# A decoder layer with routed experts: opening order, store pieces, rounding order and the summing of group 7, changed together

## What is computed

```python
x = layernorm(x + linear_attention(x))           # rotary q and k, sums over 64 tokens, W_out, + x
x = layernorm(x + cross_attention(ctx, x))       # queries from x, keys and values from ctx and x, 16 heads of 64
logits = x @ Wg + bg                             # 8 experts, the best 2 of each token, softmax over them
y_e = gelu(x @ W1[e] + b1[e]) @ W2[e] + b2[e]    # D_FF = 512
out = layernorm(x + p_1 * y_1 + p_2 * y_2)       # p_1 + p_2 = 1
```

## Time and profile before

| | |
|---|---|
| median of 3 runs | 1443.15 us (1439.3 to 1445.73) |
| the profiled execution, its own time | 1446.45 us |
| its span, first to last instruction | 1444.3 us |
| PE busy | 1382.8 us (96%) |
| ACT, DVE, POOL busy | 1171.3, 1038.3, 1000.1 us |
| share of the chain of waits on PE, DVE, "another core or an unknown queue" | 75%, 9%, 5% |
| expert tiles, from the first `hidden` to the last | 1132.3 to 1411.2 us |

### The profile page before, as it was taken

How to read it: one execution, slowest core, us unless ns; L and a number is a source line. 1 busy time by engine, 2 the same in 40 slices (tenths; PEclk the granted TensorE clock), 3 DMA queues, 4 the chain that set the end, 5 groups by cost and what they waited for, 6 DMA issues and landing times.

```text
span 1444.3 us, 37673 instructions
## 1 busy us (share of the span) xinstructions
PE 1382.8 (96%) x10833; PEld 1302.3 (90%) x10833; DVE 1038.3 (72%) x3702; ACT 1171.3 (81%) x4154; POOL 1000.1 (69%) x1543
## 2 busy tenths in 40 slices
PE   5799999999999999999999999999999989999996
PEld 4699999999999999999999999999998879988993
DVE  4566888887888887888888888787766655445664
ACT  2579999989998989998888999988987666666765
POOL 4445777777777777777777777777755554456775
PEclk9999999999999999999999999999999989999998
DMA  3211111211111211111211111127101557777894
GB/s 97 56 39 38 46 46 49 63 46 48 46 46 51 61 46 48 46 47 48 59 49 46 48 46 48 52 58 130 37 9 63 162 168 224 221 233 235 292 292 150
DMA packets 130962, 129.65 MB, mean 90 GB/s; under 512 B 11810, under 2 KB 115112, under 8 KB 130760
## 3 DMA queue, kind: packets, MB, share of 16 engines
q1 hardware_dynamic: 114328, 106.84, 26.1%
q0 software_dynamic: 8832, 16.94, 3.5%
q10 hardware_dynamic: 7600, 3.48, 0.8%
HBM read 70.83 MB, written 57.30 MB: 89 GB/s over the span
## 4 chain that ended last, share of the span: by engine, by line
PE 75%; DVE 9%; another core or an unknown queue 5%; issue 4%; ACT 3%; POOL 2%; DMA 1%; DVEq 0%; SPq 0%; ACTq 0%; POOLq 0%
PE ps_s L1633 15%; PE ps_o L1649 14%; PE ps_pT L1659 7%; PE ps_u L1688 4%; PE ps_u L1689 4%; PE ps_u L1690 4%; PE ps_t L1673 4%; PE ps_t L1670 4%; PE ps_t L1671 4%; DVE score_lo L1156 2%; ACT probs L815 2%; PE ps_t L1891 1%; PE ps_o L1891 1%; DVE wqT L1489 1%
## 5 line engine op out<-in xcount | busy, mean ns | idle before, releaser
L815 ACT ACTIVATE probs<-ps_s,neg_max 128x128 f32<-128x128 f32 x1024 | 362.7, 366 | 114.4 <-DVE neg_max L1167 114.1
L550 POOL TENSOR_TENSOR probs_n<-probs,inv_sum 128x512 f32<-128x512 f32 x256 | 267.2, 1044 | 93.8 <-DVE inv_sum L1173 91.5
L1633 PE MATMUL ps_s<-kvT,u_sb 128*128 128x128 f32 x2048 | 275.7, 278 | 0.1
L1649 PE MATMUL ps_o<-value_w,tT 128*128 128x128 f32 x2048 | 260.0, 275 | 1.1 <-ACT tT L833 1.0
L1633 PEld LDWEIGHTS ps_s<-kvT,u_sb 128*128 128x128 f32 x2048 | 254.3, 192 | 6.8 <-ACT u_sb L807 0.4
L1649 PEld LDWEIGHTS ps_o<-value_w,tT 128*128 128x128 f32 x2048 | 244.0, 192 | 1.7 <-ACT tT L833 1.4
L1178 DVE TENSOR_TENSOR pT_lo<-ps_pT,pT_hi 128x512 fp32r<-128x512 f32 x256 | 175.0, 684 | 64.9 <-ACT pT_hi L824 64.0
L694 POOL DMA_INDIRECT y_rows<-wvT,f_x x142 | 142.9, 1007 | 106.1 <-DVE wvT L1496 76.3
L563 POOL DMA_INDIRECT x_rows<-routed,pos_i x128 | 139.2, 1087 | 101.1 <-issue 93.3
L815 ACT ACTIVATION_READ_ACCUMULATOR probs<-ps_s,neg_max 128x1 f32 x1024 | 207.8, 203 | 0.0
L1167 DVE TENSOR_REDUCE neg_max<-ps_s 128x4 f32<-128x512 f32 x256 | 177.0, 691 | 34.1 <-PE ps_s L1633 25.9
(11 more groups left out here) (290 smaller groups left out, 3623.5 us busy)
## 6 DMA issues: line engine op xcount, KB each, us to landing
u_sb<-in_expert_w SPq DMA_DIRECT2D x71, 578.0 KB
x_rows<-pad_row SPq DMA_DIRECT2D x66, 520.0 KB, 4.8
f_x<-x_rows SPq DMA_DIRECT2D x71, 130.0 KB
tT<-y_rows SPq DMA_DIRECT2D x16, 512.0 KB
x_raw<-in_x SPq DMA_DIRECT2D x64, 64.0 KB, 1.7
c_raw<-in_ctx_in SPq DMA_DIRECT2D x64, 64.0 KB, 2.0
out<-value_w ACTq DMA_DIRECT2D x12, 256.0 KB, 2.5
y_rows<-wvT,f_x POOLq DMA_INDIRECT x142
```

What stands on the lines that cost most here:

```text
L550: nc.gpsimd.tensor_tensor(probs_n[:, sl], probs[:, sl], inv_sum[:, sl, :].rearrange("p (u o) -> p u o", o=1).to_broadcast([P, UP, P]), ALU ...
L815: last = nc.scalar.activation(probs[:, sl, j], ps_s[sl][:, j * P:(j + 1) * P], ACT.Exp, bias=neg_max[:, sl, j:j + 1], accum_out=sums[:, sl ...
L1633: last = nc.tensor.matmul(ps_s[sl][:, j * P:(j + 1) * P], u_sb[:, c // 2, BT * p + b, h:h + 2].rearrange("p h s -> p (h s)"), kvT[:, c, 2 ...
L1649: last = nc.tensor.matmul(ps_o[:, 0:D], tT[:, (p + 1) % 2, h], value_w[:, h], start=(h == 0), stop=(h == H - 1))
```

## The change

1. **Opening.** Scores of units 0 and 1 of the first tile move from period 0 into the opening, between pieces of folded query rows, with their `row_max`, `exps`, `inverse_sum` and the first `scale`; the preparation of tile 4 (`stats`, `in_rstds`, `in_hats`, `x_low`) moves ahead, `project(4)` and `turn_queries(4)` move into period 0.
2. **Stores.** Result row numbers are permuted so that a partition holds four rows that follow each other in the output: a store writes 2 KB per partition in one piece instead of four of 512 B. Three small instructions make the numbers in the opening.
3. **Rounding order.** For expert tiles ACT rounds the weights before the rows; DVE's `result` is split in `biased` (line 1489's work) and the rest, and DVE's order becomes `rest_weights(i + 1)`, `biased(i - 1)`, `rest_rows(i + 1)`, `result(i - 1)`. PE's `hidden` takes the low weights before the low rows. The second table of tiles (`list_rows`, `tile_rows`, `tile_table`) is made two tiles later.
4. **Group 7.** `BESIDE` = 7 groups are summed by POOL beside the tiles; group 7 joins the groups that PE sums after the last tile.

```diff
+    BESIDE = HALF_GROUPS - 1
-    IN_AT = [HALF_TILES + X_SLOTS + 7 * g // 2 for g in range(HALF_GROUPS)]
+    IN_AT = [HALF_TILES + X_SLOTS + 7 * g // 2 for g in range(BESIDE)]
-    out_z = out.rearrange("(t b) s d -> t (b s) d", b=BT)
+    out_z = out.rearrange("(g b) s d -> g (b s) d", b=ZT * BT).rearrange("g (p c) d -> g p c d", c=ZT)
...
-                sp.dma_start(out_z[bass.ds(g * ZT, ZT), :, :].rearrange("t p d -> p t d"), e_out[:, q]).then_inc(s_out[q], 16)
+                sp.dma_start(out_z[g], e_out[:, q]).then_inc(s_out[q], 16)
...
-            for i in range(NF + 5):
-                if i < NF:
-                    result_out(i)
+            for i in range(NF):
+                result_out(i)
...
-            for g in range(HALF_GROUPS, NZ):
+            for g in range(BESIDE, NZ):
                 out_rstds(g)
...
                 if i + 1 < NF:
+                    upper_weights(i + 1)
                     upper_rows(i + 1)
-                    upper_weights(i + 1)
...
-            def result(i):
-                q = i % RING
+            def biased(i):
                 dve.wait_ge(f_y_ps, i + 1)
                 dve.wait_ge(f_y_done, count(TB * i - TB))
                 nc.vector.tensor_tensor(f_yb[:, i % 2], F_Y[i % 2].rearrange("p (b d) -> p b d", d=D),
...
+            def result(i):
+                q = i % RING
                 dve.wait_ge(y_routed[q], 16 * TB * (i // RING))
...
             def ffn(i):
                 if i + 1 < NF:
-                    rest_rows(i + 1)
                     rest_weights(i + 1)
                 if i:
+                    biased(i - 1)
+                if i + 1 < NF:
+                    rest_rows(i + 1)
+                if i:
                     result(i - 1)
...
             project(2)
             turn_queries(3)
             latents_part(4)
+            score(0, 0, 0)
+            turn_x(4)
             project(3)
-            turn_x(4)
             latents_part(5)
+            latents_part(6)
+            turn_latents(2)
             make_qkv(4)
-            turn_latents(2)
-            latents_part(6)
             latents_part(7)
             turn_latents(3)
-            turn_queries(4)
+            score(0, 1, 0)
...
                 pe.wait_ge(f_xT_hi_done, i + 1)
-                pe.wait_ge(f_xT_lo_done, i + 1)
                 pe.wait_ge(f_w1_hi_done, i + 1)
-                pe.wait_ge(f_w1_lo_done, i + 1)
...
-                    nc.tensor.matmul(h, f_w1_hi[:, i % 2, part], f_xT_lo[:, i % 2], start=False, stop=False)
-                    done = nc.tensor.matmul(h, f_w1_lo[:, i % 2, part], f_xT_hi[:, i % 2], start=False, stop=True)
+                    if c == 0:
+                        pe.wait_ge(f_w1_lo_done, i + 1)
+                    nc.tensor.matmul(h, f_w1_lo[:, i % 2, part], f_xT_hi[:, i % 2], start=False, stop=False)
+                    if c == 0:
+                        pe.wait_ge(f_xT_lo_done, i + 1)
+                    done = nc.tensor.matmul(h, f_w1_hi[:, i % 2, part], f_xT_lo[:, i % 2], start=False, stop=True)
...
-            for g in range(HALF_GROUPS, NZ):
+            for g in range(BESIDE, NZ):
                 sum_rows(g)
```

More of the change, by code:

```diff
@@ L511, in _ @@
                     last_in(IN_AT.index(i))
-            for g in range(HALF_GROUPS):
+            for g in range(BESIDE):
                 if IN_AT[g] >= NF:
                     last_in(g)
-            for g in range(HALF_GROUPS, NZ):
+            for g in range(BESIDE, NZ):
                 last_in(g)
@@ L677, in _ @@
             qk_rstds(3)
+            in_rstds(4)
             z1_rstds(2)
             latent_hat(2)
-            in_rstds(4)
+            x_low(4)
             z1_rstds(3)
             latent_hat(3)
-            x_low(4)
+            scale(0, 0)
             ctx_hat(4)
@@ L736, in _ @@
                     sum_rows(SUM_AT.index(i))
-                if i - 2 in SUM_AT and i < NF - 2:
+                if i - 2 in SUM_AT:
                     out_rstds(SUM_AT.index(i - 2))
[L739 to L742, removed]
-            for g in range(HALF_GROUPS, NZ):
+            for g in range(BESIDE, NZ):
                 out_rstds(g)
@@ L859, in period @@
                 for k in range(UNITS):
-                    if on(t, 0):
+                    if on(t, 0) and (t or k > 1):
                         exps(t, k)
@@ L917, in _ @@
             keep_u(5)
+            exps(0, 0)
+            keep_u(6)
+            keep_kvT(2)
             keep_qkv(4)
-            keep_kvT(2)
-            keep_u(6)
             keep_u(7)
             keep_kvT(3)
+            exps(0, 1)
             periods(act, period)
@@ L1292, in period @@
                     return
-                if on(t, 0):
-                    row_max(0)
-                if on(t, 3):
+                if t and on(t, 0):
+                    row_max(t, 0)
+                if t and on(t, 3):
                     split_latents(t + 3)
@@ L1308, in period @@
                     z2_mean()
-                if on(t, 0):
-                    inverse_sum(0)
+                if t and on(t, 0):
+                    inverse_sum(t, 0)
                 if on(t, -4):
@@ L1320, in period @@
                     keep_prepared(EARLY + 5 if t else EARLY + 1)
-                if on(t, 0):
-                    row_max(1)
+                if t and on(t, 0):
+                    row_max(t, 1)
                 if unit_on(t, -1):
@@ L1556, in _ @@
             keep_counts(2)
+            ffn(8)
             count_tiles(2)
             then(nc.vector.tensor_tensor(list_len[:, 3], nt_f[:, 2, 1], nt_f[:, 1, 1], ALU.subtract))
-            ffn(8)
+            ffn(9)
             list_rows(1, 4)
-            ffn(9)
+            ffn(10)
             tile_rows(1, LISTS)
+            ffn(11)
             tile_table(1)
-            for i in range(10, NF + 6):
+            for i in range(12, NF + 6):
                 if i < NF:
@@ L1567, in _ @@
                 if i == NF:
+                    biased(NF - 1)
                     result(NF - 1)
@@ L1572, in _ @@
                     out_shift(SUM_AT.index(i - 4))
-            for g in range(HALF_GROUPS, NZ):
+            for g in range(BESIDE, NZ):
                 out_stats(g)
-                if g > HALF_GROUPS and g != MOST_GROUPS:
+                if g > BESIDE and g != MOST_GROUPS:
                     out_shift(g - 1)
@@ L1626, in score @@
                 n, sl, b, hf = t * 4 + k, k % 2, k // 2, k % 2
+                if k == 0 and t == 0:
+                    pe.wait_ge(u_done, 4)
+                elif k == 0 or n == 1:
+                    pe.wait_ge(u_done, 4 * t + (8 - 4 * p))
                 if k == 0:
-                    pe.wait_ge(u_done, 4 * t + (8 - 4 * p))
                     pe.wait_ge(kvT_done, 3 * t + 3)
@@ L1775, in period @@
                         out_part(t, k, p)
-                    if k == 0 and on(t, 4):
+                    if k == 0 and t and on(t, 4):
                         project(t + 4)
```

83 lines of the change are left out of this document (50 added, 33 removed).

## The result

The changed kernel takes 1507.27 us (median of 4 runs, 1505.57 to 1508.96) against 1443.49 us; the ratio is 1.0466, 95% interval 1.0429 to 1.0503. The profiled execution of the changed kernel spans 1506.0 us, 61.7 us more than that of before.

| stretch, us | before | after | difference | forecast |
|---|---|---|---|---|
| start to the first `hidden` | 1132.32 | 1129.25 | -3.1 | -4.0 |
| first 13 tiles | 59.57 | 67.99 | +8.4 | +5.5 |
| other 57 tiles | 219.35 | 277.47 | +58.1 | +44.0 |
| last `hidden` to the end | 33.06 | 31.29 | -1.8 | -4.0 |

A forecast was written before the change was run, and what follows sets the result against it. PE was taken to set the pace of the expert tiles. Terms +44.0 + 5.5 - 4.0 - 4.0 = +41.5 us, against a 1443.15 us median, gave 1485 us; range 1464 to 1512.

The forecast's parts named there:

- The closed chain: Expert tiles: PE product, DVE bias, DVE low rows, PE transposes in turn; 4.62 us a tile, +44.0 us over 57.
- product's end to the start of DVE's bias, 0.04 us: Expert tiles: first link of the chain, DVE's bias starting 0.04 us behind the end of PE's product.
- rival C: Expert tiles, much slower: PE's product message truly 1.90 us late, now on the chain; +55, about 1540 us; 8 in 100.
- The first 13 tiles: First expert tiles: 60.1 us at 4.62 us each; with a third of the old stalls kept, +5.5 us.
- small waits: Expert tiles before: the extra of a 4.26 us tile goes to these, among them 0.29 us of PE for low weights.
- the floor of 3.42 us: Expert tiles before: a tile without a stall, from product to product, takes 3.42 us.
- The opening: 40 to 80 us: PE's two longest waits, 1.71 and 2.31 us, are won; -4.0 us of 8.83 idle.
- The end: Behind the last tile: PE's 3.78 us wait for POOL's group 7 sum goes; -4.0 us with 0.2 for stores.
- The stores: Last stores at the end: longer pieces gain between nothing and 0.4 us, taken as -0.2 us.
- Rival D, the clock: Expert tiles: idle PE lowers the clock to 1.2 GHz in one tile of five; +48, about 1533 us; 5 in 100.
- Rival A: Expert tiles, faster: waiting for the product costs nothing, old stalls go; -24.4, about 1411 us in all; 7 in 100.
- B: Expert tiles, about the same: a gap near 0.57 us, total within 0.5% or 7 us; 3 in 100.

The follow-up runs named there:

- experiment 1: The change with one swap on DVE, low rows of tile i + 1 made ahead of the bias of tile i - 1: 1443.86 us, ratio to before 1.0006.
- Experiment 4: The change with POOL's two result writes of a tile direct, not indirect: 1481.39 us.
- Experiment 5: The kernel before with direct result writes, not indirect ones: 1406.57 us, ratio 0.9768.
- runs 2 and 5: Two runs on the kernel before: one with the rounding order alone, 1514.35 us; one with direct result writes, 1406.57 us.
- run 10: Opening, stores and group 7 with old tile order, paced indirect writes, sums of groups 0 to 6 on DVE, group shift one tile later: 1424.86 us, ratio 0.9884.
- experiment 8: The change with SP loading only 64 of each row's columns of expert weights from the eighth tile on: 1504.91 us, one run.

## Why the prediction was right, and where its size was off

- **The closed chain: right.** The transposes wait for the low rows in every tile, and the one swap of experiment 1 takes the loss away. The gap was put at 1.20 us between 1.10 and 1.31; with messages on time a tile takes 4.62 us, as forecast. The restart, from the transposes to the first hidden matmul, took 1251.24 - 1251.01 = 0.23 us, inside the 0.14 to 0.35 given.
- **The mis-sized term** is "product's end to the start of DVE's bias, 0.04 us", read from the earlier trace rows, a place where the message was on time. In 53 of the 57 tiles it is about 0.3 us, so a tile is 4.868 us on the mean, and 57 x (4.868 - 4.62) = 14 us were missing. That is rival C's mechanism at a sixth of its price, 0.3 us a message for 1.9: at an even pace POOL's writes do come in pairs, as argued against C, but the second one ends some 0.2 us ahead of the product's end, and there the message comes 0.3 us late. Experiment 4 gives 15.6 us back: in both runs the last of the 57 has no transposes behind it and takes 3.2 us, where the forecast counted 4.62.
- **The first 13 tiles:** +8.4 for +5.5. Experiment 4 takes 8.5 us off, so what was lost there beyond the chain is POOL's writes: 59.57 + 8.4 - 60.1 = 7.9 us, where the forecast kept a third of the stalls, 5.0, above it.
- **What I read as small waits** (0.29 us for low weights) was only the last link of what made a tile of 4.26 us. DVE's bias comes at 1254.75, 1.90 us behind the product's end, so the low rows start at 1255.81, the low weights at 1256.14, the transposes at 1256.38 and the hidden matmuls, after that wait, at 1257.08. Experiment 5 shows that the old stalls come with POOL's indirect writes, behind which the messages stood in the earlier trace rows as "remote". That made the floor of 3.42 us right, but the explanation incomplete.
- **The opening:** -3.1 for -4.0 at the first `hidden`; PE's idle time from 40 to 80 us fell from 8.83 to 5.64 us, which is about the same 3; it did not halve. But the first `hidden` starts at 1129.59 to 1132.32 us in the three profiled executions with the old opening (before, runs 2 and 5) and at 1126.15 to 1129.43 us in the nine with the new one, so executions of one opening differ by 3 us as well. DVE, which makes two of the three row-number instructions, is busy 20.46 of those 40 us, a little over half and not idle over half; no loss from them shows.
- **The end:** -1.8 for -4.0. PE's wait of 3.78 us has shrunk to 1.39 and the clock is 0.95, but the end also hangs on POOL's last result write, behind which POOL makes the next group's root, for which ACT's normalization waits. That write stood 1421.05 - 1411.24 = 9.8 us behind the last `hidden` before, and 10.2 us after; the normalization 12.4 us before and 12.7 after. One line of before, then two of after:

```profile
1423.61 1.65 ACT L940 ACTIVATE value_w<-probs_n,e_nm,e_rs 128x128 f32<-128x128 f32 x4 [9.38 <-DVE e_nm L1523]
```

```profile
1484.87 0.97 POOL L702 DMA_INDIRECT y_rows<-wvT,f_x  x1 [0.30 <-issue]
1487.42 1.50 ACT L945 ACTIVATE value_w<-ps_a,e_nm,e_rs 128x128 f32<-128x128 f32 x4 [9.23 <-DVE e_nm L1541]
```

The forecast took the longest wait for the path. With that wait shorter, the writes and then ACT are the path: from 1487.42 us on, ACT normalizes one group after another, 39.7% of the chain of waits from 1474 us, where it was 11.7% at the end of before. The 1.30 us of POOL's sum did not bring the writes forward, since POOL now waits for DVE's results (2.28 and 1.69 us ahead of the writes at 1477.08 and 1481.03).
- **The stores:** SP's last four land in 2.0 us against 2.3, ACT's in that stretch in 4.2 against 4.0: one shorter, one longer, so the 0.2 us taken for them are not shown. The Trainium skill (DMA: Bandwidth & Descriptors, Specifications) puts the least transfer for line rate at 512 B; the trace agrees in that pieces of 2 KB brought no gain that shows.
- **Rival D, the clock:** did not come. PE idles about 1.2 us in each of 57 tiles at granted clock 1.00, the level of 2.4 GHz. The halved bursts that the Trainium skill describes (TensorE: Matmul & The Clock Gate, HAM oscillation) do not follow from idle gaps of this length in this kernel.
- **Rival A** fell with the 57 waits, B with the size of the loss.

The measured 1507 lies near the top of the range, 1464 to 1512. Of the 20 us by which the spans' difference of 61.7 us exceeds the 41.5 forecast, 14 are that one link, read at a quiet place; 3 are the first 13 tiles and 3 the opening and the end.

## What to carry to other kernels

Before an instruction is moved behind a wait, follow the ring: if the waited engine's next instruction needs what is queued behind the waiter, the two engines run in turns, and the price per round is the sum of the links, which single rows of the old trace gave here to a few hundredths, but for the one that was held. Read each link at a place as busy as the one where it will stand. And when a wait's releaser is "remote" and falls behind indirect writes, try the kernel with direct ones: the difference (26 and 34 us here) is, as an estimate, the most that pacing those writes may win, since direct ones also leave POOL more time (it is busy 81.05 us of the 57 tiles in experiment 5, 131.72 before); run 10 won 18 of the 34.

## What the runs showed of the hardware

In the changed kernel, 53 of PE's 57 products end 0.14 to 0.25 us behind the end of POOL's second indirect result write, and 52 of them reach DVE 0.28 to 0.38 us behind the product's end; one that ends together with such a write comes 0.50 us late, and the other four come in 0.04 us. Before, behind four writes in a row, a message came 1.90 us late (1252.85 to 1254.75). With direct writes of the same 128 rows, to other places, every message that DVE was waiting for comes in 0.04 us, 1.7 us behind a write in experiment 4, mostly 0.63 us and in four tiles 0.03 to 0.35 us behind one in experiment 5. The load on the DMA engines is neither needed (a share of 0.30 in experiment 8) nor enough (0.87 in experiment 5).

A place just behind an indirect write is not the whole condition. In the attention part of the changed kernel, between 200 and 1100 us, 96 of PE's messages fall up to 0.5 us behind an indirect write to `x_rows`, and by the trace's semaphore updates all are on time. Whether it is the lookup of the rows' places, the scattered places themselves, the longer time that an indirect write holds POOL (0.98 us, against 1.07 us for two direct ones) or something else in it stays open.
